# A new order of the steps up to the first FFN groups, in a kernel whose whole schedule is a table of positions

## What is computed

```python
q, k, v projections of layernorm(x) and ctx by Wq, Wk, Wv   # (512 x 128), over the 128 rows
qh = softmax(qh, axis=-2) * SCALE ; kh = softmax(kh, axis=-1)
context = einsum('bhdn,bhen->bhde', kh, vh) ; out = einsum('bhde,bhdn->bhen', context, qh)
out = Wo @ out + bo ; out = out / norm(out over the rows) * g * sqrt(128)
x = x + tanh(g_xattn) * out
def bitlinear(x, w): s = mean(|w|); return x @ (round(clip(w / (s + EPS), -1, 1)) * s).T
h = layernorm(x) ; out = bitlinear(bitlinear(h, w_gate) * bitlinear(h, w_up), w_down)   # 2752 hidden
x = x + tanh(g_ffn) * out
```

## Time and profile before

| | before |
|---|---|
| median of three runs | 1386.85 us |
| profiled execution, first to last instruction (span) | 1386.2 us |
| TensorE busy | 1314.9 us (95%) |
| VectorE, ScalarE, GpSimd busy | 1003.7, 634.1, 580.5 us |
| mean granted TensorE clock, share of full | 0.979 |
| first `gu` matmul starts | 173.10 us |
| moved by DMA | 260.00 MB |

### The profile page before, as it was taken

The page is one execution under the profiler, slowest core; times in us unless marked ns, Lnnn a source line. Parts: engine busy times, 40 slices in busy tenths (PEclk is TensorE's granted clock), DMA queues, the critical chain, the costliest instruction groups (busy, mean ns, idle before and its releaser), DMA issues. The chain is left out here.

```text
span 1386.2 us, 30208 instructions
## 1 busy us (share of the span) xinstructions
PE 1314.9 (95%) x12408; PEld 961.9 (69%) x12408; DVE 1003.7 (72%) x1343; ACT 634.1 (46%) x879; POOL 580.5 (42%) x357
## 2 busy tenths in 40 slices
PE   4787599999999899999999999999999999999999
PEld 2454387855787558876598757885598748985994
DVE  6977778878799976887688875889578866641330
ACT  4668786853544424453434533453344443320220
POOL 0249925866274472444334451346034432240120
PEclk8998799999999999999999999999999999999999
DMA  9939999896664879778777975787677895663421
GB/s 352 408 145 336 267 288 306 243 184 151 146 163 99 174 180 244 182 181 186 168 176 174 196 187 136 200 169 186 150 184 181 179 171 130 159 173 88 138 76 46
DMA packets 401417, 260.00 MB, mean 188 GB/s; under 512 B 325312, under 2 KB 342080, under 8 KB 401280
## 3 DMA queue, kind: packets, MB, share of 16 engines
q1 hardware_dynamic: 394368, 232.90, 67.3%
q10 hardware_dynamic: 6912, 25.17, 5.7%
HBM read 152.37 MB, written 25.95 MB: 129 GB/s over the span
## 5 line engine op out<-in xcount | busy, mean ns | idle before, releaser
L1118 PE MATMUL ps<-w_dn,inter_buf 128*128 128x512 fp8e4 x1376 | 307.8, 380 | 2.0 <-DVE inter_buf L1372 1.3
L1118 PEld LDWEIGHTS ps<-w_dn,inter_buf 128*128 128x128 f16 x1376 | 134.9, 99 | 157.8 <-issue 4.7
L1804 POOL TENSOR_TENSOR qs<-qs,q_stat 128x1024 f32<-128x1024 f32 x64 | 129.6, 2024 | 232.9 <-DVE q_stat L1615 232.9
L1034 PE MATMUL ps<-zT,w_gu 128*128 128x256 f16 x1664 | 191.2, 274 | 3.0 <-DVE zT L1372 2.4
L1034 PEld LDWEIGHTS ps<-zT,w_gu 128*128 128x128 fp8e4 x1664 | 163.0, 99 | 29.2 <-DVE zT L1372 2.6
L1069 PE MATMUL ps<-w_gu 128*128 128x128 f16 x2880 | 174.0, 219 | 2.7 <-DVE w_gu L1715 1.8
L1069 PEld LDWEIGHTS ps<-w_gu 128*128 128x128 fp8e4 x2880 | 165.8, 98 | 7.1 <-issue 3.1
L1860 POOL TENSOR_TENSOR w_gu<-w_gu 128x512 f32<-128x512 f32 x60 | 82.4, 1373 | 179.8 <-DVE w_gu L1715 112.6
L1069 PE MATMUL ps<-zT,w_gu 128*128 128x128 f16 x2176 | 132.6, 219 | 0.0
L1715 DVE SCALAR_TENSOR_TENSOR w_gu<-ps,w_gu 128x512 f32<-128x512 f32 x120 | 82.5, 688 | 68.0 <-PE ps L1069 67.9
L1069 PEld LDWEIGHTS ps<-zT,w_gu 128*128 128x128 fp8e4 x2176 | 125.5, 98 | 3.9
(11 more groups left out here) (195 smaller groups left out, 2588.8 us busy)
## 6 DMA issues: line engine op xcount, KB each, us to landing
w_gu<-forms SPq DMA_DIRECT2D x158, 256.0 KB, 3.0
ct_raw<-forms SPq DMA_DIRECT2D x52, 256.0 KB, 3.1
w_dn<-in_down_w SPq DMA_DIRECT2D x19, 512.0 KB, 6.0
xb<-in_x ACTq DMA_DIRECT2D x16, 512.0 KB, 6.8
x_dram<-xb SPq DMA_DIRECT2D x16, 512.0 KB, 3.9
fin<-x_dram SPq DMA_DIRECT2D x32, 256.0 KB, 2.9
out<-fin SPq DMA_DIRECT2D x32, 256.0 KB, 2.4
inter_buf<-in_up_w SPq DMA_DIRECT2D x15, 512.0 KB, 9.7
```

Of the source, the lines that this page charges most:

```text
L1034: last = nc.tensor.matmul(ps[:, rest_bank(g, j), s * T:s * T + T], w_gu[:, w, k, :], zT[:, h, k, :], start=(k == 0 and h == 0), stop=(k == ...
L1118: mm = nc.tensor.matmul(ps[:, down_bank(g, k), :], inter_of(g, j, u % 2, b), w_dn[:, j, hf * 512:hf * 512 + 512], start=(u == 0), stop=(u ...
L1804: nc.gpsimd.tensor_tensor(v, v, q_stat[:, u % 2, 1, :].unsqueeze(2).broadcast_to([P, 2 * HEADS, DH]), ALU.mult).then_inc(q_prob, 1)
```

## The change

Only the table WHEN is changed; no step, wait, tile or instruction is added or taken away. The sequences differ from the start (GpSimd's from its 8th step, TensorE's from its 9th, SP's from its 54th) up to the middle of group 2: TensorE's are the same again from `product(2, 3, 2)`, which starts at 590.98 us in the trace of before, the others from steps within 15 us of that. Later numbers in the table change, but not the order that they give.

The core of the diff, first lines of the kinds that matter below:

```diff
-    "turn_k": [387, 435, 474, 514, 565, 663, 725, 775, 846, 920, 949, 974, 1076, 1109, 1167, 1239, 1270, 1322, 1373, 1418,
...
-    "kf_lo": [382, 428, 468, 511, 557, 654, 715, 769, 813, 913, 944, 971, 1070, 1104, 1148, 1235, 1265, 1314, 1366, 1415,
...
-    "zt": [353, 472],
...
-    "store_form": [290, 292, 293, 301, 1122, 1138, 1151, 1152, 1153, 1154, 1164, 1186, 1197, 1217, 1219, 1221, 1223, 1279,
...
-    "wquant": [229, 243, 245, 250, 262, 267, 270, 279, 282, 294, 299, 310, 315, 321, 326, 330, 335, 339, 345, 356, 360,
...
-    "wsign": [234, 247, 251, 259, 269, 272, 277, 283, 286, 302, 306, 319, 322, 328, 336, 341, 346, 355, 366, 371, 381,
...
+    "kf_lo": [347, 379, 468, 521, 563, 643, 706, 740, 785, 838, 928, 963, 1069, 1109, 1149, 1236, 1264, 1316, 1373,
...
+    "turn_k": [281, 282, 405, 479, 603, 645, 713, 731, 819, 860, 925, 953, 1080, 1098, 1168, 1241, 1270, 1328, 1377,
...
+    "zt": [348, 478],
...
+    "store_form": [983, 984, 1040, 1044, 1130, 1131, 1142, 1143, 1155, 1159, 1165, 1184, 1197, 1215, 1220, 1221,
...
+    "wquant": [161, 162, 205, 206, 228, 229, 242, 244, 245, 246, 247, 261, 262, 298, 299, 307, 322, 323, 324, 345,
...
+    "wsign": [278, 279, 287, 288, 302, 303, 308, 309, 310, 313, 314, 360, 361, 362, 370, 375, 376, 378, 413, 414,
```

More of the change, by code:

```diff
@@ L109 @@
[L109 to L114, removed]
@@ new lines @@
+    "turn_k": [281, 282, 405, 479, 603, 645, 713, 731, 819, 860, 925, 953, 1080, 1098, 1168, 1241, 1270, 1328, 1377,
+        1419, 1443, 1492, 1562, 1597, 1757, 1787, 1817, 1842, 1939, 1959, 1999, 2052, 2167, 2196, 2225, 2256, 2361,
+        2381, 2421, 2474, 2589, 2618, 2647, 2678, 2783, 2803, 2843, 2896, 3011, 3040, 3069, 3100, 3199, 3218, 3264,
+        3284],
+    "ctxk": [110, 155, 275, 326, 457, 581, 703, 803, 885, 991, 1161, 1250, 1350, 1433, 1557, 1626, 1810, 1866, 1993,
+        2067, 2216, 2277, 2415, 2489, 2638, 2699, 2837, 2911, 3060, 3120, 3256, 3310],
@@ new lines @@
+    "q_hi": [349, 516, 791, 976, 1185, 1423, 1668, 1898, 2108, 2266, 2530, 2688, 2952, 3110],
+    "q_lo": [305, 552, 890, 975, 1200, 1455, 1680, 1900, 2111, 2269, 2533, 2691, 2955, 3113],
[4 rows of a table added]
+    "qmax": [104, 113, 144, 145, 210, 263, 300, 301, 384, 400, 500, 530, 611, 712, 768, 810, 891, 918, 952, 980,
[3 rows of a table added]
+    "qsub": [109, 115, 147, 153, 222, 266, 316, 317, 393, 401, 535, 561, 620, 742, 796, 818, 903, 942, 967, 993,
[3 rows of a table added]
+    "qexp": [94, 121, 171, 187, 277, 291, 371, 372, 431, 432, 534, 618, 628, 780, 781, 913, 934, 961, 962, 994,
[3 rows of a table added]
@@ new lines @@
+    "turn_q": [445, 507, 636, 715, 812, 842, 897, 923, 936, 985, 1076, 1094, 1104, 1174, 1336, 1365, 1397, 1428,
+        1548, 1586, 1623, 1658, 1732, 1762, 1825, 1865, 1933, 1953, 2017, 2071, 2153, 2180, 2220, 2247, 2346, 2375,
+        2439, 2493, 2575, 2602, 2642, 2669, 2768, 2797, 2861, 2915, 2997, 3024, 3064, 3091, 3184, 3210, 3271, 3326,
+        3371, 3413],
+    "outp": [196, 197, 198, 199, 269, 270, 271, 272, 341, 342, 343, 344, 406, 407, 408, 409, 664, 665, 666, 667,
[6 rows of a table added]
+    "yev": [237, 292, 382, 420, 655, 736, 910, 951, 1071, 1135, 1322, 1394, 1534, 1622, 1733, 1799, 1934, 1979,
[3 rows of a table added]
@@ new lines @@
+    "down": [875, 876, 877, 904, 905, 915, 930, 931, 932, 933, 955, 965, 973, 990, 996, 999, 1006, 1011, 1012, 1017,
[10 rows of a table added]
+    "gcopy": [454, 469, 505, 506, 531, 538, 582, 583, 626, 627, 673, 676, 700, 702, 758, 761, 786, 792, 816, 817,
+        840, 841, 1074, 1082, 1096, 1102, 1118, 1147, 1157, 1176, 1193, 1203, 1219, 1231, 1240, 1259, 1267, 1281,
+        1291, 1306, 1317, 1344, 1361, 1369, 1519, 1541, 1969, 1983, 2397, 2408, 2819, 2830, 3239, 3250, 3521, 3528],
+    "gmul": [470, 471, 498, 499, 558, 559, 579, 580, 640, 641, 682, 683, 726, 741, 765, 766, 807, 814, 828, 829,
+        870, 874, 1070, 1081, 1105, 1111, 1127, 1152, 1169, 1190, 1204, 1210, 1225, 1242, 1251, 1269, 1271, 1288,
+        1307, 1324, 1325, 1348, 1376, 1379, 1527, 1545, 1972, 1986, 2399, 2409, 2821, 2831, 3240, 3255, 3522, 3529],
@@ new lines @@
+    "store_form": [983, 984, 1040, 1044, 1130, 1131, 1142, 1143, 1155, 1159, 1165, 1184, 1197, 1215, 1220, 1221,
+        1223, 1278, 1289, 1303, 1314, 1315, 1320, 1323, 1340, 1356, 1371, 1388, 1389, 1393, 1396, 1414, 1473, 1486,
+        1503],
+    "form": [551, 1120, 1128, 1141, 1158, 1179, 1186, 1205, 1275, 1285, 1290, 1305, 1327, 1351, 1357, 1368, 1408,
+        1469, 1477, 1493],
+    "load_form": [1513, 1515, 1517, 1520, 1522, 1524, 1526, 1529, 1554, 1568, 1573, 1576, 1579, 1584, 1591, 1602,
[11 rows of a table added]
@@ new lines @@
+    "l_hi": [62, 63, 64],
+    "l_lo": [103, 214, 264],
+    "wpart": [233, 234, 704],
+    "wtotal": [256, 257, 719],
+    "wscale": [235, 236, 723],
+    "consts": [19],
+    "prod": [17],
+    "gains": [14],
+    "wload": [25, 26, 27, 28, 29, 30, 31, 32, 33, 34, 35, 36, 37, 38, 39, 40, 41, 42, 43, 44, 55, 56, 57, 58, 59,
[5 rows of a table added]
+    "wsum": [68, 15, 16, 70, 69, 71, 72, 73, 74, 95, 97, 117, 118, 128, 129, 130, 137, 136, 140, 141, 142, 143, 151,
+        149, 156, 158, 157, 159, 172, 173, 174, 189, 203, 215, 190, 213, 217, 224, 216, 225, 226, 238, 239, 240,
+        488, 517, 540, 512, 542, 547, 541, 572, 573, 574, 589, 590, 588, 591, 592, 593, 601, 657, 674, 658, 675,
+        699],
```

228 lines of the change are left out of this document (89 added, 139 removed), and 195 rows, old and new, of the table WHEN.

## The result

The changed kernel takes 1395.43 us (median of four runs, 1394.59 to 1397.16), beside 1387.22 us for the kernel before on the same chip. The ratio is 1.0057, interval 1.0037 to 1.0077: slower, by about 8 us. The forecast was 1376, its range ended at 1388. The profiled execution has a span of 1395.4 us, 9.2 more than that of before.

What follows compares the result with a forecast made beforehand. TensorE was taken as the limit except before the first gu at 173.1 us, with DMA able to take back gains. Parts 1 to 3 gave −18, the weights' limit cut this to −11: 1386.85 − 11 = 1376 us, range 1365 to 1388.

Steps and rivals of the forecast that it cites:

- parts 1 to 3: Start to first gu: −1 up to the first rounding, −9 to yev(1, 1), −8 in the tail; together −18.
- the tail: From batch 1's last yev to the first gu: less queueing on GpSimd, VectorE and TensorE, together −8 us.
- part 2: First rounding to yev(1, 1): less ScalarE work (45.2 to 39.5 us) and six fewer GpSimd roundings; −9 us.
- Part 4: DMA give-back: gate chunk 14's load goes out at 139.4, delaying down weights; −2 to −13 us remain, −11 taken.
- the 7 that I had named as right: Sign for part 4: TensorE's waits on wsign or a transpose between 155 and 300 us grow to some 7 us.
- the 15 that would have meant a serial DMA: Sign: TensorE's waits on wsign or a transpose between 155 and 300 us over 15 us mean DMA is serial.
- the queue has no slack: Rival, chance 0.20: DMA is the bound from 140 us on; end −2, 1385 us, between 1382 and 1387.
- the figure of the Trainium skill for a transpose: 261 GB/s effective, 2.0 us or less per transpose in the DMA-heavy stretch; the give-back would vanish, about 1368 us.
- My own 2.8 us: Price of one 512 KB transpose, read from 185 GB/s moved between 300 and 303 us.
- at most the 3.0 and 6.6 idle us: Between 173 and 591 us: the most the change can gain there, from TensorE's idle time.
- The slower rival: Chance 0.12: SP blocks at turn_k(2, 0) and turn_k(2, 1) ahead of chunk 14's load; +5 to +16, 1397 us.
- the 137 from which it was to decide: End time of kf_lo(2, 1) from which SP blocking decides against the change if DMA is serial; forecast 135.

Runs made afterwards that it cites:

- old_to_gu1: Order of before up to the start of gu(1, 0, 0), new order from there on; ratio 1.0075 against the kernel before.
- new_to_gu1: New order up to the start of gu(1, 0, 0), order of before from there on; ratio 0.9996 against the kernel before.
- old_blocked: Kernel before with turn_k(2, 0) and turn_k(2, 1) put ahead of the load of gate chunk 14 on SyncE; ratio 1.0112 against the kernel before.
- light_new: Changed kernel with the first-pass loads of the down weights cut to a quarter of their columns; ratio 0.9975 against the kernel before.

## Why the prediction was wrong

**The sum of parts 1 to 3 was right, in part by luck.** Forecast −1, −9, −8, first `gu` at about 155. Measured: the first rounding at 91.56 instead of 93.53 (−2.0), `yev(1, 1)` at 139.29 (a further −6.5), and −9.7 in the tail; 154.95. The −6.5 lies just outside the bounds of part 2 (−7 to −13.5): its two work counts were 2.5 us too hopeful. The tail gained more, since `z(1, 0)` took 0.81 us where it took 2.38 before, beside a `qnorm` on GpSimd, which I had not priced:

```profile
162.12 1.90 POOL L1804 TENSOR_TENSOR qs<-qs,q_stat 128x1024 f32<-128x1024 f32 x1
```

The errors cancel. That the sum fits to 0.2 us is luck beyond that, since the same beginning of the order put the first `gu` anywhere from 153.0 to 157.2.

**Part 4 had the right cause and the wrong size and place.** The load went out at 140.27 (139.4 forecast), by two errors that cancel: `kf_lo(2, 1)` ended at 137.9, not 135, and the issue of the transpose behind it took 1.91 us, not 4.4. The last sign of a down chunk ended at 307.6 (310 forecast). I looked for the cost at the sixth part of the first `down` only and took 7 us. There it was nothing: `down(0, 0, 5)` starts at 306.69 without a wait. By then 15.9 us had been paid, most of it at `ctxk(2, 1)` and `ctxk(3, 0)`: TensorE waited 10.9 us there, between the 7 that I had named as right and the 15 that would have meant a serial DMA. By the mean clocks, 0.95 over 125.7 us and before 0.98 over 109.8, some 4 us more are half clock, an estimate. The step that failed is that the sum counts what stands in front of each load, and has no term for what the loads do to the transposes behind them; it took 4.4 us as the price of an issue. In the changed kernel it was 1.3 to 12.2 between 120 and 240 us. TensorE reached `ctxk(3, 0)` 16.7 us earlier, and its transpose left 1.7 us earlier. The case "the queue has no slack" (0.20) was nearer than the forecast: it gave −2 for the early part, and −0.84 was measured up to `gu(1, 0, 0)`. By the figure of the Trainium skill for a transpose (DMA: Bandwidth & Descriptors, section Latency and other measured facts) the give-back would have vanished; the trace went the other way, though no run here times a transpose alone. My own 2.8 us was not such a time either: from 300 to 303 us two transposes were under way, issued at 298.26 and 300.27.

**The step that decided** is the sentence that the change can gain "at most the 3.0 and 6.6 idle us" between 173 and 591 us. It bounds the gain. The next sentence allows a loss "wherever it makes TensorE stand again", but the sum has no term for the order behind 350 us, and put that loss at nothing without a reason. There the orders differ by exchanges of neighbours, and I took them for free. One on ScalarE cost 5.4 us. The late order alone costs 10.4 (old_to_gu1), and without it the kernel is level with before (new_to_gu1). VectorE was busy 247.2 of 300 us in that stretch and GpSimd 148.2 beside it; that should have given these exchanges a price on the slow side.

**The slower rival** (0.12) named the right direction and another place. Its mechanism is real (old_blocked), and the 137.9 lies past the 137 from which it was to decide if DMA is serial, but no wait for a weight chunk followed, and it is not how this kernel became slower.

## What to carry over

An exchange of two neighbours need not be free where VectorE and GpSimd are both busy: ask of every pair of neighbours that a change swaps on an engine that feeds TensorE what the delayed step will now meet. A transpose that TensorE needs soon should not be queued behind a burst of loads, and a step moved earlier on TensorE gains only what its latest transfer is moved earlier. Bound a change from below in each stretch in which the order differs at all, not only where its main gain lies.

## What the runs showed of the hardware

- The issue of a 512 KB DMA transpose on SyncE took 1.3 to 13.4 us in these traces up to 350 us. `turn_c(3, 0)`, behind a burst of six loads, took 9.2 to 13.4 in the eight kernels that order it so, and 4.2 in light_new, with the same loads cut to a quarter. `turn_q(2, 1)`, with seven loads issued in the 10 us before it, took 6.8 to 7.7, and 2.6 in light_new. The number of loads is not all: `turn_k(3, 0)` of the kernel before had seven too and took 3.8.
- A root of 128 by 4 values on GpSimd takes 1.0 to 1.2 us by itself and 3.0 when VectorE has just begun a form of 2.28 us. `z` on VectorE takes 0.8 to 3.2 us, by what GpSimd does.
- Pauses of TensorE of 4.05 and 4.25 us in group 1 were each followed by a granted clock of half (0.86 over 25 us), those of 1.61 and 1.85 us were not: the `gu` behind the 4.25 us took 3.39 us, that behind the 1.61 us took its usual 1.76.
